# Another order for the last forty feed-forward jobs of a fused attention and feed-forward kernel

## The chip, the cores and the metric

The kernel runs on one core of a Trainium2 chip. A core has TensorE (PE in the profile), which multiplies matrices into PSUM; VectorE (DVE), ScalarE (ACT) and GpSimd (POOL), which work on tiles in SBUF and, the first two, in PSUM; and SyncE (SP), which here only issues DMA transfers. POOL issues the indexed transfers. Each engine runs its own list of instructions in order, and an instruction can first wait for semaphores that other engines or transfers raise. All transfers share 16 DMA engines. The metric is the device time of one execution in microseconds (us), lower is better.

## The reference

The input is x of shape (8, 512, 2048) in float32, a context of the same shape, and weights. Cut to what matters:

```python
# part 1: residual block, per batch b
t, p, g = Wt @ ctx, Wp @ layernorm(x), Wg @ ctx          # over the 512 channels
att = sum over each of 8 groups of p * g                  # one number per group
y = grouped (64x64) Wz @ (att * t)
x = x + groupnorm(y) * gn_w + gn_b + ctx

# part 2: feed-forward over the 2048 columns, in 16 heads of 128
z = layernorm(x)[..., perm]                               # columns permuted
for h in range(16):
    out_h = gelu(z_h @ up[h]) @ down[h]                   # 128 -> 512 -> 128
x = x + out[..., unperm]
```

Every product is taken as three float32r matmuls of split operands (a high part, and the low part that is left), which gives it nearly float32 precision.

## The kernel before, in words

The eight batches are worked one after the other. Batch i has a stage S of products over x and the context, a stage Y of 192 matmuls (L848), a short stage V (L861), and then a stretch of feed-forward *jobs*. A job is one head h of one batch b: a gather by POOL brings 128 permuted rows of 512 numbers from `xg_scratch` (L1239), ACT and DVE split them (`g_hi` L972, `g_lo` L1163), PE makes the up product in two halves of 6 matmuls (`up_mm`, L887), ACT runs gelu (L979, L980), DVE takes the low part of the result (`h_lo`, L1168), PE makes the down product in two halves of 6 (`dn_mm`, L902), POOL scales and shifts the gathered rows (`resid`, L1251 and L1254), DVE adds (`add_r`, L1174), and POOL scatters the result to the output (L1259). A job is 24 matmuls in four steps of 6.

Jobs of batch b can only run once its rows are in `xg_scratch`. The rows get there at the end of part 1: DVE forms the new x in eight pieces (L1133), ACT squares them for the variance (L958), POOL takes the root (L1222, L1225), ACT normalises in place (`xln2`, L965), DVE transposes 16 blocks (`turn`, L1158) and four `store_x`, each of four transfers, write them out. For batches 0 to 6 `store_x` is issued by POOL, for batch 7 by SP (L1316), from the three RAW buffers. Scale and shift of each column are also needed in another layout: `store_sd` (L1355, eight transfers of single numbers) writes them to memory, `spread_sd` (L1363) reads them back into all partitions, into one of two buffers SM, by the parity of the batch. `resid` of batch b needs its SM buffer, and `spread_sd` of batch 7 may only overwrite that of batch 5 when the last `resid` of batch 5 is done.

The weights of a head come from memory too: 1 MB as two transfers of 512 KB by SP (`load_w`, L1337), one with the part for the up product, one with the part for the down product. There are two weight buffers WW, used in turn. A *unit* is one load of a head's weights with all the jobs that use it: a pair of jobs (two batches, same head) or a single one. A load waits until the unit two before has done its last matmul on the same half.

The jobs in a stretch are given by `units(i)`. For batch 7 it holds 40 jobs, numbered 0 to 39 here. Before the change: eight single jobs of batch 6 (heads 0 to 7), eight pairs of batches 5 and 6 (heads 8 to 15), sixteen single jobs of batch 7, so 32 units.

The order of the work on every engine is one list. `plan()` calls `put(t, stage, ...)` for every piece of work with a planned time t, sorts by t, and each engine emits its own pieces in that order. One step of 6 up matmuls and 6 down matmuls counts as 1 in t, so a job counts as 2. `f0` is the start of the jobs, `e` is `f0 + 22.8` for the last batch. Waits follow from the order; a later place in the list is also a later place behind every wait that stands ahead of it on the same engine.

Of the kernel before, what the change touches and what calls it, by code (L numbers as in the profile page):

```python
# [21 lines left out]
ND = D // P  # L22
# [4 lines left out]
TURN = [(15.9, 19.0, 22.3, 25.5)] + [(10.2, 15.0, 19.6, 24.2)] * 6  # L27
# [10 lines left out]
def units(i):  # L38

    if i == 0:  # L40
        return []
    if i == 1:
        return [(h, [0]) for h in range(8, 16)]
    half = [8 * (i % 2) + h for h in range(8)]
    if i == 2:
        half = half[6:] + half[:6]
    ws = [(h, [i - 2, i - 1]) for h in half]
    if i == B - 1:
        rest = [8 * ((i + 1) % 2) + h for h in range(8)]
        ws = [(h, [i - 1]) for h in rest] + ws + [(h, [i]) for h in range(ND)]  # L50
    return ws


# [18 lines left out]
def plan():  # L72
# [10 lines left out]
    def put(t, stage, *a):  # L83
        tasks.append((t, len(tasks), stage, a))
# [462 lines left out]
    for k in range(8):  # L547
        t = 15 + 2.6 * k
# [4 lines left out]
    for h in range(4):  # L553
        t = 38 + 4 * h
# [5 lines left out]
    base = [0, 36, 88] + [88 + 68 * k for k in range(1, B - 2)]  # L560
# [4 lines left out]
    for i in range(B):  # L565
        s0 = base[i]
        y0, v0, f0 = s0 + 16, s0 + 32, s0 + 36
# [8 lines left out]
        for dt in range(ND):  # L576
            t = s0 + (dt - 2.6 if i < 2 else S_FIRST[i > 2][dt] if dt < 4 else S_LATE.get(dt, dt - 2.6))
# [4 lines left out]
        for q in range(NQ):  # L582
            for ct in range(NT):
                t = s0 + 2.2 + 3.3 * ct + 0.8 * q if i == 2 else s0 + (4 * q + ct) * 0.85 + 0.9
                t = 10.4 + 1.4 * ct + 0.22 * q if first else s0 + 9.3 + 1.6 * ct + 0.4 * q if i == 1 else t
# [23 lines left out]
        for q in range(NQ):  # L609
            for ot in range(NT):  # L610
                put(y0 + 4 * q + ot, y_mm, i, q, ot)
            for pr in range(2):
                t = y0 + 4 * q + 2 * pr + 2
# [18 lines left out]
        last = i == B - 1  # L632
        for k in range(8):
            ct, hf = k // 2, k % 2
            t = f0 + 5 + 0.8 * k if first else f0 + 3.25 + 2 * X1_UNIT[1 if i == 1 else 2 if last else 0][k] + 0.01 * k
# [5 lines left out]
        e = f0 + 12 if first else f0 + 22.8 if last else base[i + 1] + 5.4  # L641
# [1 line left out]
        put(e + 0.1, root_x1, i)  # L643
        put(e + 0.9, shift_x1, i)
        put(e + 1.2, store_sd, i)
        put(f0 + 43 if last else f0 + 29.5 if i == 0 else e + 5, spread_sd, i)
        for ct in range(NT):
            put(e + 1.1 + (0.6 if first else 1.8 if last else 0.9) * ct, xln2, i, ct)
        for q in range(NQ):
            t = base[i + 1] + TURN[i][q] if not last else e + 5.8 + 2.6 * q  # L650
            for ct in range(NT):
                put(t + (0.6 if last else 0.25) * ct, turn, i, q, ct)
            put(t + (3 if last else 1), store_x, i, q)


        ws = units(i)
        gs = [(b, h, x) for x, (h, bs) in enumerate(ws) for b in bs]
        end = len(gs)
# [21 lines left out]
        for x, (h, bs) in enumerate(ws):  # L680
            for j in range(2):
# [3 lines left out]
                t = w_used[w + x - 2][j] if w + x > 1 else 0  # L685
                t = max(t, y0 + 7 + 2 * x) if x < 2 else t
# [27 lines left out]
def build_in(nc, ctx, x, cx, xT, cT, Wt, WpT, Wg, WzT, gnw, gnb, up, down, perm, outs):  # L714
# [3 lines left out]
    def f32(ap):  # L718
        return ap.bitcast(F32)

    order, at, free, slot, total = plan()
    S = {name: ctx.enter_context(nc.semaphore("s_" + name)) for name in total}

# [680 lines left out]
```

## Time and profile before

| | |
|---|---|
| median of 3 runs | 1599.09 us (1595.7 to 1602.59) |
| the profiled execution's own time | 1599.09 us |
| its span | 1597.3 us |
| busy: PE | 1518.1 us (95%) |
| busy: DVE, ACT, POOL | 1285.8, 974.3, 882.6 us |
| DMA | 376.87 MB, mean 236 GB/s |
| jobs of the last stretch | first up product at 1350.46 us |

The span is what the trace covers; 1.8 us of the profiled execution lie outside it. A busy PE counts only that matmuls are in flight. A row of the time line has a start, a duration, the engine, the line of the kernel, the operation with the tiles it writes and reads, and in brackets the idle time of the engine ahead of it and what ended it. SPq and POOLq rows are the issuing of a transfer, not the transfer.

### The profile page before, as it was taken

The page shows a single profiled execution, that of the slowest core. Times are in us where ns is not written, and L with a number is a line of the kernel's source. Part 1 is how long each engine was busy: PE and PEld are TensorE (multiplying, and loading weights), DVE is VectorE, ACT ScalarE, POOL GpSimd, SP SyncE. Part 2 cuts the span into 40 slices and gives each one's busy share as a digit, 9 for nine tenths or more (in the row PEclk, how much of TensorE's full clock was granted, in tenths as well). Part 3 has the DMA queues.
Part 4 walks back from the last instruction along what each step waited for, and adds up shares of the span by engine and source line. Part 5 has one row for each costly group of instructions (what it writes and reads, how often), then busy time and mean ns, then how long its engine had stood idle before and what let it go on. Part 6 is the DMA issues. An engine that isn't in the chain of part 4 may idle for free.

```text
span 1597.3 us, 19296 instructions
## 1 busy us (share of the span) xinstructions
PE 1518.1 (95%) x6592; PEld 1234.2 (77%) x6592; DVE 1285.8 (80%) x1736; ACT 974.3 (61%) x1061; POOL 882.6 (55%) x765
## 2 busy tenths in 40 slices
PE   8989899999989999899998999999999999998997
PEld 6877677877868888788877888778887788876775
DVE  5988879796996879978798797977879787878765
ACT  4325438734777257763677636775377743897875
POOL 1284537156981259712686127852378413887895
PEclk9999999999999999999999999999999999999999
DMA  8789968686675847758376773857648575769885
GB/s 324 286 297 344 286 211 318 238 296 209 219 276 186 244 149 247 271 185 264 111 253 246 215 236 120 288 219 226 209 165 273 201 248 170 257 152 267 264 283 185
DMA packets 126864, 376.87 MB, mean 236 GB/s; under 512 B 24624, under 2 KB 32816, under 8 KB 118576
## 3 DMA queue, kind: packets, MB, share of 16 engines
q1 hardware_dynamic: 92464, 253.98, 48.4%
q0 software_dynamic: 34304, 121.66, 22.5%
q8 instruction: 54, 0.88, 0.2%
q14 instruction: 42, 0.34, 0.1%
HBM read 289.55 MB, written 86.03 MB: 235 GB/s over the span
## 4 chain that ended last, share of the span: by engine, by line
PE 41%; POOL 23%; DMA 13%; DVE 10%; issue 10%; ACT 2%; SPq 1%; POOLq 0%; ACTq 0%; DVEq 0%
PE PP L848 13%; PE PP L834 12%; PE PP L902 6%; PE PP L887 6%; POOL FB L1254 5%; POOL FB L1251 5%; PE PP L861 4%; POOL out L1259 4%; DMA FB<-in_down 4%; DMA FB<-xg_scratch,perm_sb 3%; POOL FB L1239 3%; POOL WW L1200 2%; DMA xg_scratch<-FB 2%; DVE R L1168 2%; DVE R L1016 2%
## 5 line engine op out<-in xcount | busy, mean ns | idle before, releaser
L887 PE MATMUL PP<-GG,WW 128*128 128x512 f32 x1536 | 395.5, 394 | 34.5 <-DVE GG L1163 24.8
L887 PEld LDWEIGHTS PP<-GG,WW 128*128 128x128 f32 x1536 | 287.2, 189 | 106.6 <-issue 46.2
L848 PE MATMUL PP<-R,WC 128*128 128x512 f32 x1536 | 356.1, 393 | 13.7 <-DVE R L1022 7.1
L834 PE MATMUL PP<-R 128*128 128x512 f32 x1536 | 356.7, 392 | 13.0 <-DVE R L1016 11.9
L848 PEld LDWEIGHTS PP<-R,WC 128*128 128x128 f32 x1536 | 290.7, 190 | 78.0 <-issue 10.0
L834 PEld LDWEIGHTS PP<-R 128*128 128x128 f32 x1536 | 288.9, 189 | 76.1 <-issue 12.9
L902 PE MATMUL PP<-R,WW 128*128 128x512 f32 x1050 | 270.7, 393 | 8.3 <-DVE R L1168 6.4
L980 ACT ACTIVATE PP<-PP 128x1024 f32<-128x1024 f32 x256 | 261.5, 1021 | 0.0
L1168 DVE TENSOR_TENSOR R<-PP,R 128x1024 fp32r<-128x1024 f32 x175 | 213.1, 1218 | 56.1 <-ACT PP L980 55.9
L979 ACT ACTIVATE R<-PP 128x1024 fp32r<-128x1024 f32 x175 | 179.6, 1026 | 109.4 <-PE PP L887 107.9
L902 PEld LDWEIGHTS PP<-R,WW 128*128 128x128 f32 x1050 | 195.4, 189 | 55.1 <-issue 13.6
L1016 DVE TENSOR_TENSOR R<-RAW,R 128x1024 fp32r<-128x1024 f32 x128 | 168.5, 1321 | 79.5 <-ACT R L921 79.2
L1254 POOL TENSOR_TENSOR FB<-FB,SMM 128x512 f32<-128x512 f32 x128 | 208.8, 1631 | 10.1
L1245 POOL DMA_DIRECT2D xg_scratch<-FB x104 | 68.5, 670 | 252.0 <-DVE FB L1158 252.0
L1251 POOL TENSOR_TENSOR FB<-FB,SMM 128x512 f32<-128x512 f32 x128 | 167.3, 1307 | 65.8 <-DVE GG L1163 53.5
L1259 POOL DMA_INDIRECT out<-FB,perm_sb x128 | 156.1, 1220 | 85.4 <-DVE FB L1174 67.3
L921 ACT CAST R<-RAW 128x1024 fp32r<-128x1024 f32 x128 | 130.4, 1041 | 94.7 <-DMA RAW<-in_cT 45.4
L1239 POOL DMA_INDIRECT FB<-xg_scratch,perm_sb x128 | 130.4, 1019 | 97.2 <-DMA xg_scratch<-FB 35.2
L933 ACT COPY Z<-PP 128x1024 f32<-128x1024 f32 x64 | 64.8, 1013 | 153.3 <-PE PP L848 135.0
L1163 DVE TENSOR_TENSOR GG<-FB,GG 128x512 fp32r<-128x512 f32 x128 | 130.7, 1021 | 16.0 <-ACT GG L972 15.7
L1174 DVE TENSOR_TENSOR FB<-PP,FB 128x512 f32<-128x512 f32 x128 | 87.5, 684 | 60.8 <-PE PP L902 55.6
L972 ACT CAST GG<-FB 128x512 fp32r<-128x512 f32 x128 | 78.6, 614 | 75.0 <-DMA FB<-xg_scratch,perm_sb 74.8
(91 smaller groups left out, 1688.5 us busy)
## 6 DMA issues: line engine op xcount, KB each, us to landing
WW<-w_scratch SPq DMA_DIRECT2D x156, 512.0 KB
X<-in_x SPq DMA_DIRECT2D x32, 1024.0 KB, 5.6
RAW<-in_cx SPq DMA_DIRECT2D x32, 1024.0 KB
RAW<-in_xT SPq DMA_DIRECT2D x63, 512.0 KB
RAW<-in_cT SPq DMA_DIRECT2D x63, 512.0 KB
xg_scratch<-FB POOLq DMA_DIRECT2D x104, 256.0 KB, 6.1
w_scratch<-WW POOLq DMA_DIRECT2D x16, 1024.0 KB, 6.2
RAW<-in_Wg SPq DMA_DIRECT2D x8, 1024.0 KB
```

The source lines that it names most:

```text
L834: t = eng.matmul(s_bank(c1), l[:, part(c1)], r, start=(dt == 0 and j == 0), stop=(dt == ND - 1 and j == 2))
L848: t = eng.matmul(PP[2 + ot // 2][:, ot % 2, :], WC[:, l, ct, part(ot)], u[:, r + ct, :], start=(ct == 0 and j == 0), stop=(ct == NT - 1 an ...
L887: t = eng.matmul(PP[slot["up", f, p]][:, e, :], wt[:, l, part(2 * p + e)], g[:, r, :], start=(j == 0), stop=(j == 2))
L902: t = eng.matmul(PP[1][:, f % 2, :], wt[:, l, part(mt)], h_tile(f, p, r)[:, e, :], start=(mt == 0 and j == 0), stop=(mt == NM - 1 and j == 2))
L979: eng.activation(h_tile(f, p, 0), pp[:], ACT.Gelu).then_inc(S["hhi"], 1)
L980: eng.activation(pp[:], pp[:], ACT.Gelu).then_inc(S["gelu"], 1)
L1016: eng.tensor_tensor(s_tile(i, dt, 1), s_raw(i, dt), f32(s_tile(i, dt, 0)), ALU.subtract).then_inc(S["slo"], 1)
L1168: eng.tensor_tensor(h_tile(f, p, 1), PP[slot["up", f, p]][:], f32(h_tile(f, p, 0)), ALU.subtract).then_inc(S["hlo"], 1)
L1239: eng.indirect_dma_start(out=FB[:, f % NFB, :], out_offset=None, in_=xg_d[b][:, :], in_offset=perm_of(h)).then_inc(S[f"fb{f % NFB}"], 16)
L1251: eng.tensor_tensor(FB[:, f % NFB, :], FB[:, f % NFB, :], SM[b % 2][:, 0, :], ALU.mult).then_inc(S["rmul"], 1)
L1254: eng.tensor_tensor(FB[:, f % NFB, :], FB[:, f % NFB, :], SM[b % 2][:, 1, :], ALU.add).then_inc(S["radd"], 1)
L1259: eng.indirect_dma_start(out=outs[b][:, :], out_offset=perm_of(h), in_=FB[:, f % NFB, :], in_offset=None).then_inc(S[f"sc{f % NFB}"], 16)
```

## The change

The change is in the stretch of batch 7 alone. Three things are different.

The order of the jobs: the eight pairs of batches 5 and 6 come first (jobs 0 to 15), then six single jobs of batch 6 (heads 0 to 5, jobs 16 to 21), then two pairs of batches 6 and 7 (heads 6 and 7, jobs 22 to 25), then fourteen single jobs of batch 7 (jobs 26 to 39). That is 30 units where there were 32. The first job of batch 7 is now job 23, it was job 24.

The place of `spread_sd` of batch 7: planned at f0 + 30 where it was f0 + 43.

The places of the 16 transposes and four stores of batch 7: the transposes of block q are planned at e + 7.6 + 1.4 q, 0.25 apart, and were at e + 5.8 + 2.6 q, 0.6 apart; the store of block q follows 1 after its first transpose where it followed 3 after.

```diff
@@ units(i), i == B - 1
         rest = [8 * ((i + 1) % 2) + h for h in range(8)]
-        ws = [(h, [i - 1]) for h in rest] + ws + [(h, [i]) for h in range(ND)]
+        ws += [(h, [i - 1]) for h in rest[:6]] + [(h, [i - 1, i]) for h in rest[6:]]
+        ws += [(h, [i]) for h in range(ND) if h not in rest[6:]]
@@ plan()
-        put(f0 + 43 if last else f0 + 29.5 if i == 0 else e + 5, spread_sd, i)
+        put(f0 + 30 if last else f0 + 29.5 if i == 0 else e + 5, spread_sd, i)
...
         for q in range(NQ):
-            t = base[i + 1] + TURN[i][q] if not last else e + 5.8 + 2.6 * q
+            t = base[i + 1] + TURN[i][q] if not last else e + 7.6 + 1.4 * q
             for ct in range(NT):
-                put(t + (0.6 if last else 0.25) * ct, turn, i, q, ct)
-            put(t + (3 if last else 1), store_x, i, q)
+                put(t + 0.25 * ct, turn, i, q, ct)
+            put(t + 1, store_x, i, q)
```

What SP issues in the last stretch before the change, from its first weight loads on. `WW<-w_scratch` is half of a head's weights, `vq_scratch<-sd` is `store_sd`, `SMM<-vq_scratch` is `spread_sd`, `xg_scratch<-RAW` is `store_x`:

```order
L1337 DMA WW<-w_scratch 128x1024 x19
L1355 DMA vq_scratch<-sd 32x4x1 x8
L1337 DMA WW<-w_scratch 128x1024 x4
L1316 DMA xg_scratch<-RAW 32x16x128 x4
L1337 DMA WW<-w_scratch 128x1024
L1316 DMA xg_scratch<-RAW 32x16x128 x4
L1337 DMA WW<-w_scratch 128x1024
L1316 DMA xg_scratch<-RAW 32x16x128 x4
L1337 DMA WW<-w_scratch 128x1024 x2
L1316 DMA xg_scratch<-RAW 32x16x128 x4
L1337 DMA WW<-w_scratch 128x1024 x2
L1363 DMA SMM<-vq_scratch 128x1024
```

And with the change (every line number is one higher, L1338 is `load_w`):

```order
L1338 DMA WW<-w_scratch 128x1024 x11
L1356 DMA vq_scratch<-sd 32x4x1 x8
L1338 DMA WW<-w_scratch 128x1024 x3
L1364 DMA SMM<-vq_scratch 128x1024
L1338 DMA WW<-w_scratch 128x1024
L1317 DMA xg_scratch<-RAW 32x16x128 x4
L1338 DMA WW<-w_scratch 128x1024
L1317 DMA xg_scratch<-RAW 32x16x128 x4
L1338 DMA WW<-w_scratch 128x1024
L1317 DMA xg_scratch<-RAW 32x16x128 x4
L1338 DMA WW<-w_scratch 128x1024 x2
L1317 DMA xg_scratch<-RAW 32x16x128 x4
```

Eight loads fewer stand ahead of `store_sd`, and `spread_sd` has moved ahead of all four stores. The loads between the stores were those of pairs; now they are those of single jobs.

What DVE does around the first transposes before the change, from the job before them on (L1163 `g_lo`, L1168 `h_lo`, L1174 `add_r`, L1158 `turn`):

```order
L1168 TENSOR_TENSOR R<-PP,R 128x1024
L1158 STREAM_TRANSPOSE RAW<-Z 128x16x32
L1174 TENSOR_TENSOR FB<-PP,FB 128x512
L1168 TENSOR_TENSOR HX<-PP,HX 128x1024
L1158 STREAM_TRANSPOSE RAW<-Z 128x16x32 x2
L1163 TENSOR_TENSOR GG<-FB,GG 128x512
L1168 TENSOR_TENSOR R<-PP,R 128x1024
L1158 STREAM_TRANSPOSE RAW<-Z 128x16x32
L1174 TENSOR_TENSOR FB<-PP,FB 128x512
L1168 TENSOR_TENSOR R<-PP,R 128x1024
L1158 STREAM_TRANSPOSE RAW<-Z 128x16x32 x2
```

With the change the same engine has, from its first transpose on:

```order
L1159 STREAM_TRANSPOSE RAW<-Z 128x16x32 x3
L1175 TENSOR_TENSOR FB<-PP,FB 128x512
L1159 STREAM_TRANSPOSE RAW<-Z 128x16x32
L1169 TENSOR_TENSOR R<-PP,R 128x1024
L1159 STREAM_TRANSPOSE RAW<-Z 128x16x32
L1164 TENSOR_TENSOR GG<-FB,GG 128x512
L1159 STREAM_TRANSPOSE RAW<-Z 128x16x32
L1169 TENSOR_TENSOR HX<-PP,HX 128x1024
L1159 STREAM_TRANSPOSE RAW<-Z 128x16x32 x2
L1175 TENSOR_TENSOR FB<-PP,FB 128x512
L1169 TENSOR_TENSOR R<-PP,R 128x1024
L1159 STREAM_TRANSPOSE RAW<-Z 128x16x32 x3
```

The first transpose has moved behind the `h_lo` of the first half of job 15 (it stood behind that of job 14), and between two `h_lo` there are now two to four transposes where there were one or two. The order of the matmuls on PE, and that of the instructions on ACT and POOL, is the same in both kernels; only which head and batch they work on differs.

## Rows read from the trace of the kernel before

**Rows 1.** Busy time by stretch: from:to, length, PE, PEld, DVE, ACT, POOL, PEclk, DMA share, GB/s.

```profile
1360.00:1384.00 24.00, 24.00 (x108) 19.92 (x107) 21.10 (x30) 20.75 (x26) 20.87 (x18) 1.00 0.76 245
1384.00:1425.00 41.00, 39.19 (x167) 30.60 (x166) 33.56 (x37) 36.91 (x48) 37.39 (x30) 1.00 0.63 216
1425.00:1448.10 23.10, 17.72 (x72) 13.15 (x73) 14.95 (x17) 20.58 (x20) 13.84 (x13) 1.00 0.82 135
1448.10:1477.90 29.80, 28.42 (x121) 22.01 (x121) 26.98 (x33) 20.72 (x25) 25.92 (x22) 1.00 0.96 288
1477.90:1597.30 119.40, 108.06 (x468) 87.06 (x468) 78.63 (x79) 85.97 (x97) 93.65 (x77) 0.98 0.72 244
```

**Rows 2.** What PE waited for from 1300 us to the end: total, times, longest.

```profile
PE PP L887 <- DVE GG L1163: 4.9, 5, 2.5
...
PE PP L902 <- DMA WW<-w_scratch: 0.9, 2, 0.4
```

**Rows 3.** PE in order of time: start, duration, operation, and idle time ahead of it.

```profile
1385.55 1.63 PE L902 MATMUL PP<-R,WW 128*128 128x512 f32 x6 [0.43 <-DMA WW<-w_scratch]
...
1440.20 1.62 PE L887 MATMUL PP<-GG,WW 128*128 128x512 f32 x6 [2.50 <-DVE GG L1163]
...
1448.10 1.61 PE L887 MATMUL PP<-GG,WW 128*128 128x512 f32 x6 [1.27 <-issue]
...
1460.59 1.53 PE L902 MATMUL PP<-R,WW 128*128 128x512 f32 x6
...
1477.89 1.62 PE L887 MATMUL PP<-GG,WW 128*128 128x512 f32 x6 [0.52 <-DVE GG L1163]
```

**Rows 4.** POOL in order of time, the two gathers with the longest waits.

```profile
1435.88 0.97 POOL L1239 DMA_INDIRECT FB<-xg_scratch,perm_sb  x1 [3.92 <-DMA out<-FB,perm_sb]
...
1445.16 0.97 POOL L1239 DMA_INDIRECT FB<-xg_scratch,perm_sb  x1 [4.21 <-DMA out<-FB,perm_sb]
```

**Rows 5.** SP's queue in order of time: start, time of issuing, transfer, count.

```profile
1425.27 3.94 SPq L1355 DMA_DIRECT2D vq_scratch<-sd  x8
...
1449.88 3.89 SPq L1316 DMA_DIRECT2D xg_scratch<-RAW  x4
1453.94 1.48 SPq L1337 DMA_DIRECT2D WW<-w_scratch  x1
1456.47 4.36 SPq L1316 DMA_DIRECT2D xg_scratch<-RAW  x4
1460.99 1.82 SPq L1337 DMA_DIRECT2D WW<-w_scratch  x1
```

**Rows 6.** DVE in order of time, five entries of job 16 in a row.

```profile
1451.49 1.28 DVE L1158 STREAM_TRANSPOSE RAW<-Z 128x512 f32<-128x512 f32 x2
1452.70 0.79 DVE L1163 TENSOR_TENSOR GG<-FB,GG 128x512 fp32r<-128x512 f32 x1
1453.41 1.22 DVE L1168 TENSOR_TENSOR HX<-PP,HX 128x1024 fp32r<-128x1024 f32 x1
1454.55 0.70 DVE L1158 STREAM_TRANSPOSE RAW<-Z 128x512 f32<-128x512 f32 x1
1455.18 0.65 DVE L1174 TENSOR_TENSOR FB<-PP,FB 128x512 f32<-128x512 f32 x1
```

**Rows 7.** The 16 transposes of batch 7 on DVE: ns min/median/max, first and last start.

```profile
L1158 DVE STREAM_TRANSPOSE RAW<-Z x16: 669/693/703, 1442.1 to 1472.8; 128x512 f32<-128x512 f32 x16
```

**Rows 8.** Two short stretches by the columns of the first group.

```profile
1430.00:1435.00 5.00, 5.00 (x23) 4.08 (x23) 3.09 (x4) 5.00 (x5) 1.80 (x2) 1.00 0.77 46
...
1460.00:1465.00 5.00, 4.89 (x22) 3.65 (x20) 4.92 (x7) 2.36 (x4) 3.52 (x5) 1.00 1.09 346
```

**Rows 9.** The chain that ended last: start, duration, what it went through.

```profile
1468.01 8.17 DMA FB<-xg_scratch,perm_sb
...
1556.25 7.12 DMA WW<-w_scratch
...
1565.11 1.36 PE PP L887 x6
```

## The prediction, written before the changed kernel was run

> **What bounds the kernel now.** I read the busy times by stretch first, then PE's waits and its time line in the last stretch, and then the queues that feed it: POOL, SP, DVE. PE is the bound: a step of six matmuls takes 1.36 us when nothing is late [rows 9], a job of four steps 5.44 us, and the page has PE 95% busy. The change can only move what PE loses in the last stretch, so the question is where that is. From 1360 to 1384 us PE is busy all the time and DMA is at 0.76 [rows 1]: the single jobs of batch 6 that the change takes away from there cost PE nothing. From 1384 to 1425 it loses 1.8 us, of which 0.43 us are one wait for weights [rows 3]; the rest is the pace of POOL, 37.4 of 41 us busy. From 1425 to 1448.1 it loses 5.4 us, from 1448.1 to 1477.9 another 1.4 by busy time, and by its pace more: jobs 16 to 20 take 1477.89 - 1448.10 = 29.8 us against 5 x 5.44 = 27.2, so 2.6 us. After that the losses are small: both waits for weights from 1300 us on sum to 0.9 us [rows 2], and one of them is the early one.
>
> The 5.4 us have their cause ahead of any transfer that the change touches. SP issues the eight transfers of `store_sd` at 1425.3 to 1429.2 [rows 5]. From 1430 to 1435 the DMA engines are 0.77 busy and move 46 GB/s [rows 8], POOL waits 3.92 and 4.21 us for old scatters to free a buffer, and the gather behind them makes PE wait 2.50 us [rows 3, 4]. The jobs at that place are pairs before and after the change, so this loss stays. The Trainium skill (DMA: Bandwidth & Descriptors, the opening table) gives 512 bytes as the least piece that moves at line rate and says that smaller ones are read, modified and written. These pieces are 4 bytes; the trace agrees with its 46 GB/s. By that rule fewer weight loads nearby would not shorten the stall.
>
> **The change part by part.**
>
> *Two units fewer.* Four loads of 512 KB go, 2.1 MB of 376.87. That is worth time only where PE waits for weights: at most the 0.9 us of [rows 2]. The early wait of 0.43 us goes (the jobs there become pairs), but POOL's pace is right behind it, so I count 0 to -0.4. In the tail 14 single jobs stand where 16 stood, and PE loses some 0.4 us there to weights: 0 to -0.4. Together -0.5, and no more than -0.9.
>
> *Earlier `spread_sd`.* It needs `store_sd` landed and the last `resid` of batch 5, job 14's, which with the new order is done by then. It costs 0.5 MB of DMA at about 1441 instead of 1488, in the stall. Between 0 and +1.5 us; I take 0, and keep the rest for the range.
>
> *Transposes on DVE.* All 16 stood from 1442.1 to 1473 [rows 7]; three ran while PE was stalled anyway, the others over five jobs. Now the first stands behind the `h_lo` of job 15's first half, which ends at about 1449.2, and all 16 follow within five halves of jobs. By the starts of [rows 6] a transpose takes 0.61 us of DVE, `h_lo` 1.14, `g_lo` 0.71 and `add_r` some 0.6. In the new order: `h_lo` of job 15's second half ready at 1449.2 + 4 x 0.61 + 0.6 + 1.1 = 1453.3; job 16's two at about 1456.4 and 1459.3; job 17's two at 1463.6 and 1467.1; then DVE has its slack back. PE reached the first down step of job 17 at 1460.59 [rows 3], so by DVE alone it would be 3.0 us late there and, with the pace of before, some 2.7 us late at job 20.
>
> *Stores and weight loads on SP.* This is the large term. SP issues in order, and a store of four transfers keeps it for 3.9 to 4.4 us, the weight load right behind for 1.5 to 1.8 [rows 5]. Before, the loads between the stores were those of pairs, needed only every 10.9 us. Now jobs 16 to 21 are single, and a weight buffer has only about 6.8 us (five steps) between the end of its last use and its next. A load needs about 7.1 us from issue to landing, from the one load on the chain [rows 9] (bounds: nothing below the 3 us or so that 512 KB would take alone at half of the 346 GB/s of [rows 8], nothing above the 8.2 us that a gather takes in the same stretch). The walk:
> - Store 0 when its transposes are done, 1452.2, issued by 1456.3; the up half for job 18 by 1457.8.
> - Store 1 when its transposes are done, 1457.6, so SP is held until 1462.0. Behind it stands the down half for job 17, whose buffer was free at about 1454.7. It is issued at 1462 to 1463.5 and landed at 1469 to 1470.
> - PE takes the first down step of job 17 at about 1469.8 instead of 1460.6.
> - Store 2 until 1468, then the up half for job 19 and the down half for job 18, issued by 1470.5, landed 1476 to 1477.5. Store 3 until 1475, then the up half for job 20, issued by 1476.5, landed at 1483.
> - PE: job 17's down step 1469.8, job 19's up step 1475.8, job 18's down step 1477.3, job 20's up step 1483, and job 21 starts 5.44 us later, at 1488.3 instead of 1477.9: +10.4 us. This holds the 2.7 us of DVE, which runs beside it.
>
> The same by volume: jobs 16 to 20 as single jobs need 5 x 0.52 = 2.6 MB more weights than as pairs, and `spread_sd` adds 0.5. DMA is already at a share of 0.96 in this stretch with 288 GB/s [rows 1]; 3.1 MB more at the 346 GB/s of its fullest 5 us [rows 8] is 9.0 us, less some 3 us for gaps at its start. So +6 by volume, +10.4 by queueing. I take +9.5, since both act, but some landings will be quicker than 7.1 us.
>
> Sum: +9.5 - 0.5 = +9.0. Against the profiled execution's own 1599.09 us, which is also the median of the runs, that is 1608. The late jobs can't win it back: PE and, by the same trace, POOL run there at the pace of the jobs.
>
> **The rivals.**
>
> *DVE alone.* If SP's loads land before PE needs them, the transposes remain: +2.7 - 0.5, 1601. For it: PE never waited for weights between the stores before, and the trace shows no landing time of a single load there. Against it: with pairs it could not have waited, there were 10 us in hand.
>
> *Gathers starve too.* The gathers and scatters of POOL share the DMA engines with stores and loads. In this stretch a gather took 8.17 us [rows 9], and in the stall two old scatters held POOL for 8.1 us [rows 4]. If stores, single loads and gathers pile up, POOL is held once or twice more by some 3 to 4 us each, on top of my sum, about 6: 1614. The Trainium skill (Trainium Kernel Development and Optimization, Key Constraints) says that transfers issued from SP, ACT and POOL run on the same 16 DMA engines and interleave. By that rule this cost would be real even though POOL has its own queue; the trace agrees with the 8.17 us.
>
> *Faster.* The place is jobs 16 to 20 again. The price of before there is 2.6 us, spent on four stores spread over 27 us, each of which holds up gathers. If the cost of a store is fixed by its place between gathers rather than by bandwidth, packing the four into some 22 us, with transposes that come later, could clear the way sooner: -2.6 - 0.9, and perhaps 1 us of the stall, so -4.5: 1594.5. It decides at job 21: this case holds if PE gets from job 16 to job 21 in under 29.8 us. For it: two weight units less, and DMA at 0.72 after 1477.9. Against it: the share of 0.96 before, with half the weights.
>
> *A late batch 7.* Its first job is now 23, its gather is issued with job 20. If the stores land after that, POOL waits; but the same hold on SP delays job 20 as well, so I give it no time of its own.
>
> **How the numbers follow.** SP's queue decides (1608, own range 1604 to 1613): 0.52. Gathers starve too (1614): 0.18. DVE alone (1601): 0.18. Faster (1594.5): 0.12. Likeliest 1608. The range is 1596 to 1617: it cuts the lower end of the faster case and the far end of the starving one. A measurement of this kernel can tell about 0.5%, 8 us: slower means over 1607.1, faster under 1591.1. Of the main case two thirds lie above 1607.1 (0.35), of the starving one all (0.18): slower 0.53. Faster by over 8 us needs the stall around `store_sd` to shrink as well: 0.05. Same: 0.42.
>
> **What would show it.** PE's waits in the changed kernel should have a new entry of several us for weights at the down step (L903) and the up step (L888), in jobs 17 to 20, 1460 to 1490 us. SP's queue should show the down half for job 17 issued right behind store 1, many us after its buffer was free. DVE should be full from 1449 to 1468. The stall from 1425 to 1448 should be as before, within 1.5 us. From job 22 on the pace should be 5.44 us. I am wrong if PE goes from job 16 to job 21 in under 32 us, or if the new loss is in waits for gathers with the weights in time, or if the stretch ahead of 1448 changes by more than 2 us.

## The result, and the profile after

| | before | changed |
|---|---|---|
| median of 8 runs each | 1600.37 us | 1611.01 us |
| ratio, 95% interval | | 1.0078 [1.0058, 1.0098] |
| span of the profiled execution | 1597.3 us | 1605.9 us |
| job 0 starts at | 1350.46 us | 1346.13 us |
| jobs 0 to 11 | 68.23 us | 68.24 us |
| jobs 12 to 15 | 29.41 us | 28.78 us |
| jobs 16 to 20 | 29.79 us | 45.95 us |
| jobs 21 to 25 | 28.25 us | 27.20 us |
| job 26 to the last down step | 80.04 us | 78.48 us |
| from there to the end | 11.12 us | 11.12 us |

The change makes the kernel slower by 0.78%, some 12.5 us. (The medians of the eight runs in the table are 10.6 us apart; over all 21 timed runs of the changed kernel the median is 1612.5 us.) A row of jobs goes from the first up step of its first job to that of the next row's first job. The spans differ by only 8.6 us, because the stages ahead of job 0, which the change leaves as they are, happened to take 4.3 us less in the one profiled execution. In the ten profiled kernels here with that part unchanged and in the changed one itself job 0 starts anywhere from 1346.1 to 1358.7 us. So I compare from job 0 on: 246.84 us before, 259.77 after, +12.9, which fits the ratio. It is one place: jobs 16 to 20 cost 16.2 us more, and everything else gives 3.2 back.

Busy time by stretch of the changed kernel, by the columns of [rows 1]:

```profile
1360.00:1384.00 24.00, 24.00 (x107) 19.90 (x106) 20.34 (x26) 20.78 (x27) 21.56 (x18) 1.00 0.54 175
1384.00:1425.00 41.00, 39.02 (x166) 30.23 (x164) 32.66 (x36) 37.40 (x47) 37.02 (x31) 1.00 0.54 162
1425.00:1448.10 23.10, 18.21 (x74) 13.05 (x72) 15.35 (x17) 20.53 (x21) 14.52 (x13) 1.00 0.76 187
1448.10:1477.90 29.80, 20.98 (x74) 15.56 (x75) 19.87 (x27) 13.29 (x16) 19.80 (x17) 0.83 0.95 288
1477.90:1500.00 22.10, 19.16 (x78) 15.09 (x77) 11.21 (x13) 14.19 (x17) 13.05 (x12) 0.92 0.76 251
```

The fourth row answers to the fourth of [rows 1]: PE is busy for 21.0 us where it was 28.4, and runs 74 matmuls where it ran 121, while DMA has the same share and the same 288 GB/s. So PE starved at a rate of transfers that fed it before. But five single jobs also need more bytes than five jobs of pairs: rate times length gives 8.6 MB for jobs 16 to 20 before and 11.9 MB in the changed kernel (259 GB/s over 45.95 us, the row is shown with the experiments). At 288 GB/s 11.9 MB take 41 us, so an unchanged rate doesn't clear the DMA engines. The granted clock, third from the end, is new too: 0.83 here and 0.92 in the next row, where [rows 1] have 1.00 and 0.98.

What PE waited for in the changed kernel from 1300 us on, as in [rows 2]:

```profile
PE PP L888 <- DVE GG L1164: 5.1, 5, 2.5
PE PP L903 <- DMA WW<-w_scratch: 4.2, 2, 3.8
PE PP L888 <- DMA WW<-w_scratch: 4.2, 2, 2.1
```

PE in order of time, from job 16 (1443.15) to job 21 (1489.10), to be held against [rows 3]:

```profile
1443.15 1.63 PE L888 MATMUL PP<-GG,WW 128*128 128x512 f32 x6 [2.59 <-issue]
...
1458.45 2.35 PE L888 MATMUL PP<-GG,WW 128*128 128x512 f32 x6 [2.10 <-DMA WW<-w_scratch]
1464.61 2.90 PE L903 MATMUL PP<-R,WW 128*128 128x512 f32 x6 [3.81 <-DMA WW<-w_scratch]
1467.31 2.49 PE L888 MATMUL PP<-GG,WW 128*128 128x512 f32 x6
...
1473.28 1.62 PE L888 MATMUL PP<-GG,WW 128*128 128x512 f32 x6 [2.08 <-DMA WW<-w_scratch]
...
1481.52 1.66 PE L888 MATMUL PP<-GG,WW 128*128 128x512 f32 x6 [2.53 <-DVE GG L1164]
1483.59 2.90 PE L903 MATMUL PP<-HX,WW 128*128 128x512 f32 x6 [0.41 <-DMA WW<-w_scratch]
...
1489.10 1.52 PE L888 MATMUL PP<-GG,WW 128*128 128x512 f32 x6
```

SP's queue of the changed kernel over the four stores, in the columns of [rows 5]:

```profile
1447.67 3.59 SPq L1317 DMA_DIRECT2D xg_scratch<-RAW  x4
1451.37 0.58 SPq L1338 DMA_DIRECT2D WW<-w_scratch  x1
1452.90 4.04 SPq L1317 DMA_DIRECT2D xg_scratch<-RAW  x4
1457.10 1.90 SPq L1338 DMA_DIRECT2D WW<-w_scratch  x1
1459.04 6.11 SPq L1317 DMA_DIRECT2D xg_scratch<-RAW  x4
1465.26 3.49 SPq L1338 DMA_DIRECT2D WW<-w_scratch  x2
1468.80 3.95 SPq L1317 DMA_DIRECT2D xg_scratch<-RAW  x4
1472.85 3.31 SPq L1338 DMA_DIRECT2D WW<-w_scratch  x2
```

The load at 1457.10 is the down half for job 17. It stands right behind store 1, and PE takes that step at 1464.61, 21.5 us after job 16 began; before it was 12.5 [rows 3]. The loads at 1465.26 follow store 2, and PE waits 2.08 us at 1473.28. Those at 1472.85 follow store 3. The first of them is the up half for job 20. The wait of 2.53 us at 1481.52, which the trace puts down to the low part `g_lo`, is very likely this load's: the two loads landed 8.3 and 8.5 us after their issue, so at about 1481.3 the first, and the `g_lo` that ends just then (1480.79 + 0.68) is by the order of the list that of job 21, not of job 20. A wait is named after what came last, and here two things came within 0.2 us. With it the waits for weights are 2.10 + 3.81 + 2.08 + 2.53 + 0.41 = 10.9 us of the 18.75 by which jobs 16 to 20 exceed 5 x 5.44.

The clock in three 4 us stretches of the changed kernel, same columns as the busy times above:

```profile
1456.00:1460.00 4.00, 1.91 (x7) 1.30 (x6) 4.00 (x7) 1.53 (x2) 3.54 (x3) 0.89 1.07 363
1460.00:1464.00 4.00, 0.80 (x2) 0.08 (x1) 4.00 (x6) 1.94 (x2) 2.40 (x3) 0.50 1.05 345
1464.00:1468.00 4.00, 3.39 (x8) 2.74 (x9) 0.56 (x1) 0.00 (x0) 2.12 (x2) 0.50 1.01 312
```

After the two waits of 2.10 and 3.81 us the granted clock is 0.50, which is 1.2 GHz. A group of six then takes 2.90 us instead of 1.52. The groups at 1458.45, 1464.61, 1467.31 and 1483.59 are 0.8 + 1.4 + 1.0 + 1.4 = 4.6 us too long. So the 18.75 us are 10.9 for weights, 4.6 of clock, 1.1 of waiting for ACT in job 16 and 2.1 of small gaps; before, small gaps and waits were 2.6. Waits and clock are not fully apart: a slow group ahead of a late load only shortens the wait for it.

### The profile page after: what moved, and what is told of

Read it like the earlier page. It is cut to its first block, busy times and chain, and to the rows that moved or that the text cites. A ratio compares the mean times of both kernels' runs of the same rounds, so it can differ in the third digit from the quotient of the medians.

```text
span 1605.9 us, 19290 instructions
## 1 busy us (share of the span) xinstructions
PE 1518.3 (95%) x6592; PEld 1234.1 (77%) x6592; DVE 1279.0 (80%) x1736; ACT 974.7 (61%) x1061; POOL 874.1 (54%) x765
## 2 busy tenths in 40 slices
DMA packets 126288, 374.77 MB, mean 233 GB/s; under 512 B 24560, under 2 KB 32752, under 8 KB 118000
## 4 chain that ended last, share of the span: by engine, by line
PE 45%; POOL 17%; DVE 17%; DMA 10%; issue 7%; ACT 3%; SPq 0%; POOLq 0%; DVEq 0%; ACTq 0%
PE PP L835 14%; PE PP L849 13%; PE PP L903 7%; PE PP L888 6%; POOL FB L1255 5%; PE PP L862 5%; POOL FB L1252 4%; POOL out L1260 4%; DMA FB<-xg_scratch,perm_sb 3%; DVE R L1017 3%; POOL FB L1240 2%; DVE X L1029 2%; DMA WW<-w_scratch 2%; DVE R L1169 2%; DVE Z L1134 2%
## 5 line engine op out<-in xcount | busy, mean ns | idle before, releaser
L835 PE MATMUL PP<-R 128*128 128x512 f32 x1536 | 360.7, 394 | 18.0 <-DVE R L1017 16.2
L1255 POOL TENSOR_TENSOR FB<-FB,SMM 128x512 f32<-128x512 f32 x128 | 202.9, 1585 | 10.1
L1252 POOL TENSOR_TENSOR FB<-FB,SMM 128x512 f32<-128x512 f32 x128 | 166.9, 1304 | 63.5 <-DVE GG L1164 50.6
L1164 DVE TENSOR_TENSOR GG<-FB,GG 128x512 fp32r<-128x512 f32 x128 | 122.9, 960 | 11.8 <-ACT GG L973 11.5
L903 PE MATMUL PP<-HX,WW 128*128 128x512 f32 x486 | 125.1, 393 | 0.4 <-DMA WW<-w_scratch 0.4
```

Source lines behind the costliest of these rows:

```text
L835: t = eng.matmul(s_bank(c1), l[:, part(c1)], r, start=(dt == 0 and j == 0), stop=(dt == ND - 1 and j == 2))
L903: t = eng.matmul(PP[1][:, f % 2, :], wt[:, l, part(mt)], h_tile(f, p, r)[:, e, :], start=(mt == 0 and j == 0), stop=(mt == NM - 1 and j == 2))
L1252: eng.tensor_tensor(FB[:, f % NFB, :], FB[:, f % NFB, :], SM[b % 2][:, 0, :], ALU.mult).then_inc(S["rmul"], 1)
L1255: eng.tensor_tensor(FB[:, f % NFB, :], FB[:, f % NFB, :], SM[b % 2][:, 1, :], ALU.add).then_inc(S["radd"], 1)
```

## The experiments

The theory is that of the prediction: SP issues in order, and the weight loads of single jobs stand behind stores that hold SP for 4 to 6 us. Its rivals: the bytes themselves (volume, which the prediction counted as acting beside the queue); the density of the transposes on DVE; the backlog of the `store_sd` stall just ahead; the new place of `spread_sd`. Ratios are against the kernel before, measured on the same chip; a hundredth of a per cent is 0.16 us. "Jobs 16 to 20" is from the one profiled execution, 29.79 before and 45.95 in the changed kernel. How far one execution can stray is seen in jobs 12 to 15: in the nine other profiled kernels that keep the old `store_sd` they take 26.2 to 30.1 us.

**The transposes and stores alone**, in the order of jobs of before.

```diff
-            t = ... e + 5.8 + 2.6 * q
+            t = ... e + 7.6 + 1.4 * q
-                put(t + (0.6 if last else 0.25) * ct, turn, i, q, ct)
-            put(t + (3 if last else 1), store_x, i, q)
+                put(t + 0.25 * ct, turn, i, q, ct)
+            put(t + 1, store_x, i, q)
```

> The kernel before with one part of the change alone: the transposes and stores of batch 7 at the new, tighter places; order of the jobs and the place of spread_sd as before, so the jobs beside the stores are pairs. Theory 'loads held by SP' (weights that single jobs need at once stand in SP's queue behind the stores): pairs have some 10 us in hand, so little is lost, 0 to +3 us against before, and PE waits for weights under 1 us in all. Rival 'DVE' (the dense transposes are the cost): +3 us or more, in waits for DVE. Rival 'tight stores fill the DMA engines': most of the change's +12 us shows here too.

Measured: 1607.31 us, 1.0045 [1.0027, 1.0064]; jobs 16 to 20 take 37.23. A miss: 7.2 us by the ratio where 0 to 3 were expected, and 3.1 us of waiting for weights where it was under 1. Pairs do not protect the loads once the stores are close together. SP's queue and, below it, PE:

```profile
1459.00 5.09 SPq L1316 DMA_DIRECT2D xg_scratch<-RAW  x4
1464.25 2.33 SPq L1337 DMA_DIRECT2D WW<-w_scratch  x1
```

```profile
1472.43 2.90 PE L887 MATMUL PP<-GG,WW 128*128 128x512 f32 x6 [3.08 <-DMA WW<-w_scratch]
1475.13 2.76 PE L902 MATMUL PP<-HX,WW 128*128 128x512 f32 x6
1477.69 1.96 PE L887 MATMUL PP<-GG,WW 128*128 128x512 f32 x6
```

One load behind store 2 is 3.08 us late, and the clock adds 1.4 + 1.2 + 0.4 = 3.0.

**The jobs alone**: the changed order of jobs, transposes and stores at their old places, `spread_sd` at f0 + 30 as changed.

```diff
-            t = ... e + 7.6 + 1.4 * q
+            t = ... e + 5.8 + 2.6 * q
-                put(t + 0.25 * ct, turn, i, q, ct)
-            put(t + 1, store_x, i, q)
+                put(t + (0.6 if last else 0.25) * ct, turn, i, q, ct)
+            put(t + (3 if last else 1), store_x, i, q)
```

> The changed kernel with the transposes and stores of batch 7 back at their places of before, wide apart; the new order of the jobs and the early spread_sd stay. Theory 'loads held by SP': single jobs still meet the stores, but two of the four stores now have the next loads ahead of them, and the transposes fit into DVE's slack: +4 to +9 us against before, with waits for weights of 2 to 6 us; the gather of job 23 now stands right behind the last store and may add 1 to 3 us. Rival 'DMA volume': about as much as the change, +11 to +13, since the same bytes move in the same jobs. Rival 'DVE': under +2.

Measured: 1606.99 us, 1.0048 [1.0030, 1.0066]; jobs 16 to 20 take 43.05. PE's waits over them:

```profile
PE PP L903 <- DMA WW<-w_scratch: 6.3, 3, 5.7
PE PP L888 <- DMA WW<-w_scratch: 4.0, 2, 2.8
```

The 7.7 us of the ratio are in the expected range; the 10.3 us of waits for weights (2 to 6 expected) and the +13.3 us of this one profile are not. Each part alone costs about 0.45 to 0.48%, both 0.78%.

**The loads ahead of stores 1 to 3**, in the changed kernel.

```diff
-            put(t + 1, store_x, i, q)
+            put(f0 + (31.4, 33.1, 35.1, 37.1)[q] if last else t + 1, store_x, i, q)
```

> The changed kernel with one thing different: the second, third and fourth store of batch 7 are placed behind the weight loads that are free to go at that point (planned at f0 + 33.1, 35.1 and 37.1 where they were at 32.8, 34.2 and 35.6). Bytes, transposes and jobs are those of the change. Theory 'loads held by SP': the down half for job 17 is issued some 5 us sooner, PE's waits for weights fall from 8.4 us to under 3, the time falls by 5 to 10 us against the change, so it is 2 to 7 us over before. Rival 'DMA volume': no more than 2 us better than the change. Rival 'DVE': no difference.

Measured: 1611.41 us, 1.0081 [1.0059, 1.0103]; jobs 16 to 20 take 40.71. No gain in the time, where 5 to 10 us were expected, though the stretch in the profile is 5.2 us shorter than the changed kernel's. The waits for weights are 6.8 us, not under 3. This is the outcome that the volume rival had foretold, and that of DVE. PE, then SP:

```profile
1467.32 2.72 PE L888 MATMUL PP<-GG,WW 128*128 128x512 f32 x6 [3.25 <-DMA WW<-w_scratch]
...
1484.16 1.24 PE L888 MATMUL PP<-GG,WW 128*128 128x512 f32 x3 [2.92 <-DMA WW<-w_scratch]
```

```profile
1458.73 2.69 SPq L1338 DMA_DIRECT2D WW<-w_scratch  x2
1461.47 6.19 SPq L1317 DMA_DIRECT2D xg_scratch<-RAW  x4
1467.76 2.52 SPq L1338 DMA_DIRECT2D WW<-w_scratch  x2
```

The down halves are in time now and the up halves late. With two loads just issued ahead of it, a store holds SP for 6.19 us. One queue holds both kinds, and here the order within it only chose which was late.

**Pairs beside the stores**: six single jobs of batch 6 first, then the eight pairs, then the rest as changed, so still 30 units; transposes at their old places, stores 0.8 earlier.

```diff
-        ws += [(h, [i - 1]) for h in rest[:6]] + [(h, [i - 1, i]) for h in rest[6:]]
+        ws = [(h, [i - 1]) for h in rest[:6]] + ws + [(h, [i - 1, i]) for h in rest[6:]]
-        put(f0 + 30 if last else ...
+        put(f0 + 39.6 if last else ...
+            put(t + (2.2 if last else 1), store_x, i, q)
```

> The new set of jobs in another order: the six single jobs of batch 6 first, then the eight pairs of batches 5 and 6, then the two pairs of batches 6 and 7 and the fourteen single jobs. It has the change's 30 units and its first job of batch 7 at 23, but pairs beside the stores; transposes at the places of before, each store 2.2 behind its first transpose, spread_sd at f0 + 39.6. Theory 'loads held by SP': nothing of the change's loss, -3 to +2 us against before. Rival 'fewer units are themselves the gain, their place is not': the same. Rival 'the early batch 7 costs' (gather of job 23 right behind the last store, its scale read back late): +3 to +6 us, in waits of POOL.

Measured: 1600.01 us, 1.0010 [0.9996, 1.0025]; jobs 16 to 20 take 28.96 with no wait for weights. The place of the single jobs is what cost: this kernel differs from the one with the jobs alone (1.0048) mainly in that, and has the transposes wide apart like it. The loss is gone and nothing is gained: jobs 21 to 25 take 31.83 where they took 28.25. POOL and PE there:

```profile
1478.77 0.97 POOL L1240 DMA_INDIRECT FB<-xg_scratch,perm_sb  x1 [4.78 <-DMA xg_scratch<-RAW]
```

```profile
1486.88 2.65 PE L888 MATMUL PP<-GG,WW 128*128 128x512 f32 x6 [2.77 <-DVE GG L1164]
```

The first gather of batch 7 is one job earlier than before and waits 4.78 us for the last store. That is the "late batch 7" to which the prediction gave no time; it shows once the other wait is away.

**Half the bytes**: twelve weight loads in jobs 16 to 21 bring only the high parts, 256 KB instead of 512. The low parts are left out.

```diff
+                if 56 <= w <= 61:
+                    eng.dma_start(... WW[w % 2][:, 2 * j:2 * j + 1, :] ...)
+                    continue
```

> The changed kernel, but the twelve weight loads of the six single jobs of batch 6 (jobs 16 to 21) bring only the high part, 256 KB each instead of 512; the low part is left out and PE multiplies what is in the buffer. That takes 3.1 MB from the stretch beside the stores, which is what the new order of the jobs had added; number, order and place of the loads stay. Theory 'the DMA engines are full' (so each store holds SP long, and each load lands late): PE's waits for weights fall from 8.4 us to under 3, the time is 6 to 10 us better than the change. Theory 'SP's order alone' (the loads stand behind stores that wait for transposes): no more than 3 us better.

Measured: 1606.17 us, 1.0041 [1.0024, 1.0057]; jobs 16 to 20 take 41.61.

```profile
PE PP L903 <- DMA WW<-w_scratch: 5.4, 1, 5.4
PE PP L888 <- DMA WW<-w_scratch: 4.3, 3, 2.0
```

In this profile half the bytes take 4.3 of the 16.2 us away, and PE still waits 9.7 us for weights: three stores still held SP for 5.19, 5.21 and 3.66 us. By the times they give back more, 1.0078 - 1.0041, which is 5.9 of the 12.5 us. That lies between the two expectations (no more than 3 us for the queue alone, 6 to 10 for full engines). Volume is a part, and nothing here makes it the smaller one.

**More bytes**: before, with six further copies of 512 KB, memory to memory, behind the loads of three units beside the stores.

```diff
+                if 60 <= w <= 62:
+                    eng.dma_start(jk_d[w - 60, :, 2 * j:2 * j + 2, :], w_d[h, :, 2 * j:2 * j + 2, :])...
```

> The kernel before, where SP also copies, right behind each of the six weight loads of three pairs beside the stores (jobs 16 to 21), the same 512 KB within memory, to a place that nobody reads: 3.1 MB more through the DMA engines in that stretch, while the weights are still those of pairs with 10 us in hand. Theory 'the DMA engines are full': +5 us or more against before, in waits for weights and gathers. Theory 'single jobs need their loads at once, behind the stores': 0 to +3 us.

Measured: 1605.41 us, 1.0023 [1.0003, 1.0044]. Busy times over jobs 16 to 20 and behind:

```profile
1452.00:1480.20 28.20, 27.55 (x119) 22.00 (x120) 26.71 (x35) 22.05 (x27) 24.70 (x20) 1.00 1.02 319
1480.20:1514.00 33.80, 29.84 (x124) 23.67 (x123) 20.84 (x21) 22.98 (x27) 24.48 (x21) 0.95 0.83 269
```

319 GB/s where 288 were moved [rows 1], and jobs 16 to 20 take 28.28 us, less than before. So DMA was not full at 288 GB/s. But the experiment puts less into this stretch than was meant. SP issues two of the six copies before job 16 starts (at 1437.17 and 1445.23 us, job 16 at 1452.23) and the last at 1477.09. By rate times length jobs 16 to 20 move 9.0 MB where before has 8.6 and the changed kernel 11.9. Jobs 21 to 25 take 33.41 us for it, in waits behind late gathers and in a fall of the clock, not in waits for weights. From job 16 to job 26 that is 3.7 us more than before, the same as the ratio, and between the two expectations. It doesn't show that the engines could carry the volume of the change without a loss.

**The loads off SP**: in the changed kernel ACT issues the loads of the five units beside the stores (two loads each); SP keeps the stores.

```diff
+            elif stage == "load_w" and 57 <= a[0] <= 61:     # in ACT's list
+                ...
+                eng.dma_start(f32(WW[w % 2]...), w_d[h, ...])...
```

> The changed kernel, but the ten weight loads for jobs 17 to 21 are issued by ScalarE, at the same places of the list, so that they no longer stand behind the stores on SP; all bytes and the stores stay. Theory 'SP's order': the down half for job 17 is issued when its buffer is free, waits for weights fall to under 3 us, 6 to 10 us better than the change. Theory 'the DMA engines are full': loads are issued early but land as late, no more than 3 us better. ACT may lose 1 to 2 us of its own by waiting for the down steps.

Measured: 1606.90 us, 1.0044 [1.0027, 1.0060]; jobs 16 to 20 take 38.50. PE's waits and, below, DVE:

```profile
PE PP L903 <- DVE HX L1176: 4.3, 1, 4.3
...
PE PP L903 <- DMA WW<-w_scratch: 0.7, 1, 0.7
PE PP L888 <- DMA WW<-w_scratch: 0.3, 1, 0.3
```

```profile
1467.34 1.31 DVE L1166 STREAM_TRANSPOSE RAW<-Z 128x512 f32<-128x512 f32 x2 [4.25 <-DMA xg_scratch<-RAW]
```

The waits for weights fall from 10.9 to 1.0 us, with every byte still moved, and the down half for job 17 is issued 7.3 us after the start of job 16 instead of 13.95. That is the clearest sign for the queue. The time is 5.4 us better by the ratios, a little under the 6 to 10 expected, and about what half the bytes gave. Against the changed kernel's own interval this one's just touches; the next kernel, run on the same chip and nearly the changed one, took 1613.11. Of the 9.9 us 4.3 are taken back at once: the transposes of block 3 need the RAW buffer of block 0, there are three, and its store has not landed; DVE stands 4.25 us, and behind the transpose stands the `h_lo` that PE needs. The clock takes 2.4 us more after that wait.

Jobs 16 to 20 in the changed kernel, with half the bytes and with the loads off SP, by the columns of [rows 1]:

```profile
1443.15:1489.10 45.95, 33.87 (x120) 24.81 (x121) 28.45 (x37) 23.38 (x28) 28.77 (x25) 0.85 0.83 259
1448.04:1489.65 41.61, 30.62 (x121) 23.01 (x122) 28.46 (x37) 23.46 (x28) 28.90 (x25) 0.96 0.82 234
1447.61:1486.11 38.50, 31.34 (x121) 23.53 (x121) 28.82 (x38) 23.87 (x28) 25.19 (x22) 0.91 0.96 309
```

They move 11.9, 9.7 and 11.9 MB. With the loads off SP the DMA share is back at 0.96, and the stretch is still 8.7 us longer than before. With half the bytes the share is 0.82, and it is 11.8 us longer. So the queue delays PE with engines to spare, and without the queue the engines run as full as before on 3.3 MB more. Both act, as the prediction had it, and what either costs alone overlaps with the other.

**`spread_sd` later**, in the changed kernel: `put(f0 + 38 ...` instead of `f0 + 30`.

> The changed kernel with spread_sd planned at f0 + 38 instead of f0 + 30, so behind the four stores; its 512 KB leave the stall around store_sd. Both theories: 0 to -1.5 us against the change, since a term of 0 to 1.5 us was given to it. If it is more than 3 us better, the early spread_sd is a cause that I had put at nothing. If it is slower, spread_sd behind the stores holds loads or the resid of job 23.

Measured: 1613.11 us, 1.0070 [1.0046, 1.0095]; jobs 16 to 20 take 45.34. Its place costs nothing that can be measured; the interval leaves room for some 5 us either way.

**Dense transposes, stores where they were**, in the order of jobs of before.

```diff
+            t = ... e + 7.6 + 1.4 * q
+                put(t + 0.25 * ct, turn, i, q, ct)
+            put(e + 8.8 + 2.6 * q if last else t + 1, store_x, i, q)
```

> The kernel before with the 16 transposes of batch 7 at the tight places of the change, but its four stores where they were before (so SP's queue is as before). Against e1_turns_alone (+0.45%), where the stores were tight too, it tells DVE from SP. Theory 'dense transposes cost PE by DVE': +2 to +4 us against before, in waits for DVE. Theory 'only the tight stores cost, by what stands behind them on SP': 0 to +1 us.

Measured: 1603.44 us, 1.0022 [1.0006, 1.0038]; jobs 16 to 20 take 31.72, +1.9, with no wait for weights. PE's waits there are 0.5 us for DVE and 1.1 for ACT, the rest small gaps, so the 3.5 us of the ratio are in the expected range but not mainly in waits for DVE. So DVE's part of the first experiment's 0.45% is about half by the ratios (by the stretch, 1.9 of 7.4 us), the stores on SP the rest.

**The stall of `store_sd` away, before and changed.** DVE transposes the 128 x 8 scales and shifts for each batch, and the eight transfers of `store_sd` write runs of 128 bytes instead of 4.

```diff
+        put(e + 1.5, flip_sd, i)
-        put(e + 1.2, store_sd, i)
+        put(e + 1.6, store_sd, i)
+                eng.transpose(sdt[:], sdp[:])                      # flip_sd, on DVE
-                      eng.dma_start(vq_d[...].rearrange("(c r) -> r c", r=32), sd[32 * r:32 * r + 32, k, :])
+                      eng.dma_start(vq_d[...].rearrange("(c r) -> c r", r=32), sdt[32 * r + 4 * k:32 * r + 4 * k + 4, :])
```

> The kernel before, in all batches: DVE first transposes the 32 x 32 blocks of the tile that store_sd writes (one more transpose of 128 x 32 per batch), so that each of its eight transfers writes 4 pieces of 128 bytes in place of 128 pieces of 4. Theory 'the stall from 1425 to 1448 is the 1024 small writes': the stall of batch 7 falls from 5.4 us of idle PE to under 1.5, the time is 4 to 8 us better than before. Rival 'the stall is the root and the normalising on POOL, DVE and ACT': 0 to -1 us.

> The changed kernel with the same transposed store_sd. Theory 'the change's loss is SP's order in jobs 16 to 21, apart from the stall': it is better than the change by as much as g1_flip_before is better than before, and the loss between the two stays 10 to 14 us. Rival 'the stall leaves a backlog on the DMA engines that makes the loads late': the loss between the two falls by 4 us or more.

Measured: on the kernel before 1588.70 us, 0.9927 [0.9899, 0.9955]; on the changed one 1606.37 us, 1.0034 [1.0017, 1.0051]. In the first, the 5 us that begin some 4 us after `store_sd`, to be held against the first of [rows 8], and POOL's gather there against [rows 4]:

```profile
1425.00:1430.00 5.00, 4.96 (x22) 3.74 (x20) 3.08 (x4) 5.00 (x5) 4.60 (x4) 1.00 0.91 297
```

```profile
1431.74 1.36 POOL L1254 DMA_INDIRECT FB<-xg_scratch,perm_sb  x1 [0.30 <-issue]
```

297 GB/s where it was 46, and up to job 16 no gather waits for a buffer, where two waited 8.1 us together. PE is idle for 2.3 us of the 23.1 us from 1420.5 on; before it was 5.4 of the same length [rows 1], and under 1.5 was expected. Jobs 12 to 15 take 26.03 us (26.02 and 26.04 in the two other kernels with the new `store_sd`) instead of 29.41. But with the old one they can take 26.2 as well, so the waits of POOL are clearly the small writes' doing, and what they cost PE in one execution is anything from 0.2 to 4 us.

The gain on the kernel before is 11.7 us (4 to 8 expected), on the changed one 7 us. The change now costs 1.0034 / 0.9927 = 1.0108, so 17 us where 10 to 14 were expected, and jobs 16 to 20 take 45.52. With the stall gone the loss did not shrink, so it is not the backlog of the stall. The kernel before with the new `store_sd` is the fastest of all that ran.

**The two together**: six single jobs first, with the new `store_sd`.

> e4_six_first (six single jobs first, then pairs, 30 units) with the transposed store_sd: the version that the experiments point to. 4 to 8 us better than before, within 1.5 us of g1_flip_before: its two units less are worth under 1 us, and its early job of batch 7 waits for the last store.

Measured: 1595.48 us, 0.9973 [0.9957, 0.9988]. Better than before by the 4 us expected, but 7 us behind the new `store_sd` alone, where 1.5 were expected: jobs 21 to 25 take 32.94 us where they take 27.77 there, by the late batch 7 again.

## Why the prediction was right, and which term was mis-sized

The forecast was 1608 with slower likelier than same; it is 1611, slower. The place, the queue and the order of events were as predicted. The time came as near as it did because two errors have opposite signs: the stretch of jobs 16 to 20 lost 6.7 us more than the term of 9.5, and the jobs around it gave back 2.7 more than the 0.5 foreseen. By its steps:

- *Stall ahead stays, within 1.5 us*: jobs 12 to 15 went from 29.41 to 28.78. Right, though other kernels with the same work at that place vary by 4 us. That POOL's waits come from the transfers of 4-byte numbers was argued then, and the new `store_sd` has shown it. The Trainium skill (DMA: Bandwidth & Descriptors, the opening table), cited there, puts line rate at 512 bytes a piece; no run here tried that size for these numbers, and the waits for buffers went already at 128.
- *Two units fewer, -0.5*: DMA moved 374.77 MB, 2.1 less. Jobs 12 to 15 and 21 on took 3.2 us less together. One us of it is waits of PE behind the start of job 21, 1.7 before and 0.7 now. Not much of it need be the two units: the kernel with the transposes and stores alone has all 32 units, and takes 2.6 us less than before in the same jobs. The prediction said that the late jobs can't win anything back, and they did; why is open.
- *`spread_sd`, 0*: nothing speaks against it in the experiment that moved it.
- *Transposes, +2.7 beside the rest*: DVE ran without a gap from 1444.56 to 1464.6 us, as foretold, then idled 6.67 us for PE. Alone they cost 1.9 us at this place, 3.5 by the ratio. About right.
- *SP's queue, +10.4 by the walk, taken as +9.5*: measured +16.2 for the stretch. This is the term that was mis-sized. Counted from job 16's start, the walk has the load of job 17's down half issued at +13.9, and it was +13.95; PE at that step at +21.7, and it was +21.5. It fails after that. Store 2 held SP for 6.11 us where 4.4 were taken from [rows 5], and the two loads behind it took 3.49 where the walk has 2.5; job 20's up step came at +38.4 instead of +34.9, so 3.5 of the missing 5.8 us were lost by then. From there to job 21 it was 7.6 instead of 5.4: another wait of 0.41 and a group at half the clock, 1.4. The walk had no term for the clock at all.
- *By volume, +6*: 3.3 MB more moved, 3.1 foreseen. The term was rather too small: with the loads off SP the stretch is 8.7 us longer than before at a DMA share of 0.96, though 4.3 us of that are the wait behind DVE; half the bytes gave back 4.3 us in the profile and 5.9 by the ratio.

*DVE alone* is out: PE waited 10.9 us for weights. *Gathers starve too* is out, though its 1614 is as near to the time as my 1608. In jobs 16 to 20 POOL waited for PE's results by way of `add_r`, not for buffers or transfers:

```profile
1472.20 1.02 POOL L1260 DMA_INDIRECT out<-FB,perm_sb  x1 [6.00 <-DVE FB L1175]
```

*Faster* is out by the 45.95 us. *Late batch 7* was hidden, as argued, and costs 3.6 and 5.2 us in jobs 21 to 25 of the two kernels where the rest is mended.

What stays open: how the 16.2 us split between hold of SP and slower landing. The loads landed after a median of 7.0 us, up to 8.5. Off SP the down half for job 17 was issued in time and its step began 8.9 us later, after 0.71 us of waiting for it, so the landings did not get faster. The split can't be read from two experiments that each change both.

## What to carry to other kernels

A single job needs its weights every 5 us, and an in-order queue that also carries stores of many small pieces must be reckoned as the sum of its holds, each at the length it has when the transfers are at their fullest. Put work with slack (here pairs, needed every 11 us) beside such stores, and keep the stores apart: close together they made even a pair's load 3.08 us late. A queue of their own for the loads took nearly all waits for weights away but needs more buffers for the stores too; whether it then wins was not tried. And count the bytes per job before blaming the queue: at the rate of before the bytes of five single jobs alone take 41 us. And look at the smallest pieces first: 4 KB written as 4-byte numbers in each batch were worth 0.73% in the kernel before and 0.4% in the two others, which is more than any reordering here won.

## What the hardware showed that I had not expected

- The hold of a store on SP is no constant. Four transfers of 256 KB took 3.59 us of SP at a DMA share of 0.82 and 6.11 at 1.07 in the changed kernel, 6.19 at 0.92 with the loads placed first, and 7.81 at 1.01 with the extra copies. A weight load behind a store took 0.58 us or 1.90. With half the bytes two stores still held SP for 5.2 us each, at a share of 0.92 and 0.93.
- PE's granted clock falls to 0.50 (1.2 GHz, six matmuls in 2.90 us instead of 1.52) after waits of 2.1 and 3.8 us close together, and in other kernels after one of 2.7, 3.1 or 4.3 us. The wait of 2.50 us before [rows 3] left it at 1.00, and one of 2.50 us ahead of job 16 with the loads placed first did not (the next group took 2.90 us). So the length of the last wait alone does not decide it. Each such fall adds 1.4 to 3.2 us.
- The cost of extra traffic can show up behind the place where it is moved: 319 GB/s at a DMA share of 1.02 passed with PE busy for 27.55 of 28.20 us, and the 5.2 us were lost in the five jobs after it. A DMA share of 0.96 [rows 1] was no proof that DMA set the pace there.
